# A two-layer attention and FFN kernel on one core: one fixed instruction order replaced by another

## What is computed

```
q, k, v = xs @ Wq, xs @ Wk, xs @ Wv                 # per segment of 128 tokens
sq, sk = elu(q) + 1, elu(k) + 1
att_mem = sq @ mem / (sq @ z)                       # the memory before this segment
mem, z = mem + sk.T @ v, z + sum(sk)                # carried from segment to segment
att = gate * att_mem + (1 - gate) * softmax(q @ k.T / 8) @ v
x = layernorm(x + att @ Wo)
x = layernorm(x + relu(x @ Q(W1).T + b1) @ Q(W2).T + b2)
# Q(W) = clip(round(W / (mean|W| + 1e-5)), -1, 1)
```

## Time and profile before

| | us |
|---|---|
| median of 3 runs | 1915.3 (1911.3 to 1917.6) |
| the profiled execution | 1912.87 |
| its span | 1910.9 |
| PE busy | 1855.7 (97%) |
| DVE busy | 1449.1 (76%) |
| ACT busy | 1006.1 (53%) |
| POOL busy | 794.7 (42%) |

### The profile page before, as it was taken

One profiled execution on the slowest core, in us unless ns is written; L12 is line 12 of the kernel. 1 busy time (PEld: TensorE's weight loads), 2 busy tenths in 40 slices (PEclk: granted clock), 3 DMA queues, 4 the chain that ended last, 5 costly groups with the idle time before them and its releaser, 6 DMA issues.

```text
span 1910.9 us, 44707 instructions
## 1 busy us (share of the span) xinstructions
PE 1855.7 (97%) x16575; PEld 1311.8 (69%) x16575; DVE 1449.1 (76%) x2969; ACT 1006.1 (53%) x2426; POOL 794.7 (42%) x790
## 2 busy tenths in 40 slices
PE   5689999999999999999999999999999999999998
PEld 3566677766777766677766677766677766677765
DVE  7867777777777787777777877777777777777774
ACT  5755555555554555554555554545555645555541
POOL 1813344443344444344444344444345444344443
PEclk9889999999999999999999999999999999999999
DMA  8412333223333233233223333323333322333110
GB/s 270 123 23 46 58 61 66 52 49 59 62 59 65 49 53 61 58 60 65 54 45 64 61 59 64 64 38 60 61 59 63 67 38 59 61 58 62 36 23 23
DMA packets 556422, 117.49 MB, mean 61 GB/s; under 512 B 529824, under 2 KB 533808, under 8 KB 555696
## 3 DMA queue, kind: packets, MB, share of 16 engines
q1 hardware_dynamic: 556208, 114.64, 29.4%
HBM read 50.54 MB, written 16.80 MB: 35 GB/s over the span
## 4 chain that ended last, share of the span: by engine, by line
PE 80%; SPq 7%; DVE 6%; DMA 3%; issue 2%; ACT 1%; POOL 1%; DVEq 0%; POOLq 0%; ACTq 0%
PE bank L431 12%; PE bank L430 12%; PE bank L444 8%; PE bank L445 8%; SPq L1551 7%; PE bank L280 6%; PE bank L282 6%; PE bank L281 6%; PE bank L413 3%; PE bank L411 3%; PE bank L412 3%; PE bank L368 3%; DMA amax_row<-amax_dram 2%; PE bank L294 2%; PE bank L347 2%
## 5 line engine op out<-in xcount | busy, mean ns | idle before, releaser
L430 PE MATMUL bank<-yt,w1t 128*128 128x256 f16 x2048 | 453.9, 273 | 0.0
L431 PE MATMUL bank<-yt,w1t 128*128 128x256 f16 x2048 | 453.9, 273 | 0.0
L1141 ACT ACTIVATE prob<-bank,exp_bias,gscalars 128x128 f32<-128x128 f32 x512 | 227.6, 455 | 356.6 <-DVE exp_bias L723 347.7
L444 PE MATMUL bank<-w2t,arena 128*128 128x512 f16 x1024 | 388.4, 379 | 0.0
L445 PE MATMUL bank<-w2t,arena 128*128 128x512 f16 x1024 | 388.1, 379 | 0.0
L1187 ACT ACTIVATE arena<-bank,b_scaled,wscalars 128x256 f32<-128x256 f32 x512 | 262.9, 569 | 213.4 <-PE bank L431 156.3
L858 DVE CAST arena<-arena 128x512 f16<-128x512 f32 x256 | 154.8, 605 | 89.9 <-ACT arena L1187 89.1
L1317 POOL TENSOR_TENSOR att_mem<-att_mem,gate_in 128x512 f32<-128x512 f32 x60 | 83.1, 1385 | 330.1 <-DVE att_mem L762 318.7
L430 PEld LDWEIGHTS bank<-yt,w1t 128*128 128x128 f16 x2048 | 200.5, 98 | 23.3 <-issue 0.3
L431 PEld LDWEIGHTS bank<-yt,w1t 128*128 128x128 f16 x2048 | 200.3, 98 | 22.7
L1395 POOL TENSOR_TENSOR arena<-arena 128x512 f16<-128x512 f32 x128 | 155.3, 1213 | 87.6 <-DVE arena L858 87.6
(11 more groups left out here) (191 smaller groups left out, 4392.9 us busy)
## 6 DMA issues: line engine op xcount, KB each, us to landing
rows<-in_L_attn_x SPq DMA_DIRECT2D x32, 512.0 KB, 3.6
out_rows<-rows SPq DMA_DIRECT2D x64, 256.0 KB, 2.3
x_blocks<-in_L_attn_x SPq DMA_DIRECT2D x248, 64.0 KB, 2.8
sk<-sk_t SPq DMA_DIRECT2D x480, 32.0 KB, 2.0
att_dot<-att_mem SPq DMA_DIRECT2D x480, 32.0 KB, 2.0
y_blocks<-rows SPq DMA_DIRECT2D x480, 32.0 KB
arena<-in_L_ffn_W SPq DMA_DIRECT2D x6, 1024.0 KB, 5.5
w2t<-in_L_ffn_W SPq DMA_DIRECT2D x2, 1024.0 KB, 13.3
```

The costliest lines, as they stand in the source:

```text
L430: pe.matmul(ps[:, c], w1t[:, k, cols], yt[:, g % 2, :, k], start=k == 0, stop=False)
L431: ins = pe.matmul(ps[:, c], w1t[:, k, cols], yt[:, g % 2, :, KT + k], start=False, stop=k == KT - 1)
L444: pe.matmul(banks[own][:], h_hi[:, f, toks], w2t[:, f, :], start=f == 0, stop=False)
L1141: ins = act.activation(prob[:, t, at], ps[:, c], ACT.Exp, scale=gcol(g, G_EXP), bias=exp_bias[:, t, at:at + 1], accum_out=row_sum[:, t, h: ...
```

## The change

The five engines' loops are written in another order. No instruction is added or removed, with one exception that is no work: DVE's `turn_x` now also waits for the maximum of the same group, which stands ahead of it in the same queue. Line numbers of the changed kernel are one or two off.

The core of the diff, cut to the parts that matter for the steps below:

```diff
+                dve.wait_ge(sem["amax"], g + 1)
                 dve.transpose(x_blocks[:, t], x_blocks[:, t]).then_inc(sem["xturn"], 1)
...
+                if g == 0:
+                    turn_max(1)
+                    spread_max(1)
                 ffn_up(g - 2, 1)
...
+                if g == 1:
                     for n in range(0, 4):
                         turn_w(n)
...
+                read_memory(g, 1)
+                ffn_up(g - 1, 0)
                 attend(g, 1)
-                ffn_up(g - 1, 0)
```

More of the change, by code:

```diff
@@ L548, in _ @@
+                scores(g, 0)
+                project_out(g - 1, 1)
+                ffn_down(g - 2, 0, 0)
                 project_v(g, 0)
-                ffn_down(g - 2, 0, 0)
+                ffn_down(g - 2, 0, 1)
                 project_v(g, 1)
+                scores(g, 1)
+                turn_p(g, 0, 0)
                 if g == 0:
                     turn_bias_max()
-                turn_p(g, 0, 0)
-                ffn_down(g - 2, 0, 1)
+                ffn_down(g - 2, 0, 2)
+                turn_y(g - 1, 0)
@@ L568, in _ @@
+                turn_y(g - 1, 1)
                 turn_p(g, 1, 1)
+                attend(g, 0)
                 ffn_down(g - 2, 1, 2)
[L570 to L573 removed]
                 ffn_down(g - 2, 1, 3)
[L575 to L578 removed]
                 read_memory(g, 1)
[L580 to L585 removed]
+                ffn_up(g - 1, 0)
@@ L1014, in _ @@
                     threshold(1)
-                p_split(g, 0, 0)
-                v_split(g, 1)
-                score_max(g, 1, 0)
-                read_scale(g, 0)
                 score_max(g, 1, 1)
-                residual(g - 2, 0, 1)
                 if g == 0:
@@ L1023, in _ @@
                         compare(n)
+                p_split(g, 0, 0)
+                residual(g - 2, 0, 1)
+                scale_sums(g, 0)
+                read_scale(g, 0)
+                p_split(g, 0, 1)
+                normalise(g - 2, 0, 1)
+                turn_y(g - 1, 0)
+                if (g + 1) % (LIVE * NSEG) < LIVE and LIVE * NSEG <= g + 1 < NG:
+                    reset_memory((g + 1) // (LIVE * NSEG), place(g + 1)[2])
+                yt_lo(g - 1, 0)
+                turn_y(g - 1, 1)
+                p_split(g, 1, 0)
+                yt_lo(g - 1, 1)
+                all_max(g + 1)
+                att_scale(g, 0)
+                x_scale(g + 1, 0)
+                p_split(g, 1, 1)
+                read_scale(g, 1)
+                x_scale(g + 1, 1)
                 invert_sums(g, 1)
-                scale_sums(g, 0)
+                x_scale(g + 1, 2)
+                if g == 0:
+                    scalars(0, 3)
+                x_scale(g + 1, 3)
                 scale_sums(g, 1)
-                turn_y(g - 1, 0)
-                all_max(g + 1)
-                p_split(g, 0, 1)
-                x_scale(g + 1, 0)
+                scalars(g + 1, 0)
+                att_scale(g, 1)
+                scalars(g + 1, 1)
+                h_split(g - 1, 0)
+                xt_lo(g + 1, 0)
+                scalars(g + 1, 2)
                 if g == 0:
@@ L1051, in _ @@
                         compare(n)
-                att_scale(g, 0)
-                read_scale(g, 1)
+                residual(g - 2, 1, 1)
                 if g == 0:
@@ L1227, in _ @@
             for g in range(NG + 2):
+                if g == 1:
+                    for n in range(12, 16):
+                        put_w(n)
                 if g == 0:
-                    w_sum(1, 1)
-                h_relu(g - 2, 4)
+                    gates()
+                h_relu(g - 2, 1)
+                h_relu(g - 2, 2)
+                if g == 0:
+                    w_split("v", 0)
+                if g == 1:
+                    for n in range(16, 20):
+                        put_w(n)
+                if g == 0:
+                    w_split("v", 1)
+                qk_split(g, "k", 0)
+                h_relu(g - 2, 3)
                 if g == 1:
@@ L1276, in _ @@
                         put_w(n)
-                p_split(g, 1, 0)
-                yt_hi(g - 1, 0)
+                xt_hi(g + 1, 1)
                 if g == 0:
@@ L1617, in _ @@
                     load_x(1)
+                move_att(g)
+                if g == 0:
+                    load_ffn_w(2, 2)
                 put_out(g - 2, 1)
```

310 lines of the change are left out of this document (134 added, 176 removed).

## The result

| | before | changed |
|---|---|---|
| median | 1915.3 us (5 runs, 1911.3 to 1917.6) | 1936.1 us (5 runs, 1934.7 to 1936.8) |
| ratio | | 1.0116, 95% interval 1.0099 to 1.0133 |
| profiled execution, its span | 1912.87, 1910.9 | 1936.11, 1934.2 |
| late excess in 28 periods | 9.9 us | 2.7 us |
| undisturbed period | 56.77 us | 57.63 us |

A second comparison of the same two kernels gave 1.0121 (1.0106 to 1.0136): 1936.2 against 1912.5. The forecast of 1907 and its range up to 1917 both missed.

What follows compares the result with a forecast made beforehand. PE, busy for 97% of the span, was taken as the bound, with a 56.77 us floor per group. 1912.9 - 9.5 (late landings) + 3.5 (opening) = 1907 us; range 1901 to 1917.

Steps and rivals of the forecast that it cites:

- (b): Turn of the group: ACT's relu(0), both xt_hi and relu(1) in a row cost PE nothing, with 0.45 us slack.
- (c): Other moved waits (memory add, k and q splits, at_lo, h_rest): 0.9 us or more of slack each, costing nothing.
- The slower rival: At the group's turn a late x_scale delays ACT's relu(1); PE waits 0.6 us in all 30 groups: 1925 us, chance 0.08.
- (a) The landing: DVE reads the returned maximum later, behind p_split(1,0), so late DMA transfers stop delaying groups: gain 9.5 us.
- The 0.4 allowed for leftovers: Part of the 9.9 us late-group excess expected to remain after DVE reads the returned row later: 0.4 us.
- (d) The opening: Before the regular groups: later first k projection and slower turning of FFN weights, costing 3.5 us, bounds -1 and +9.
- the cheap opening: Rival: POOL compares alone in the opening, each falling from 1.97 to 1.57 us; 1901.5 us, chance 0.10.
- (e) The tail: Last two turns, without k, q, v: PE always fed, so no cost, 0 to 1 us.

## Why the prediction was wrong

**The floor of a period: the step that failed.** "Since the change moves instructions and removes none, 56.77 us stays the floor of a group." It rose by 0.87. Two terms were missing.

First, 0.53 us from steps (b) and (c). Step (b), on the turn of the group, prices ACT and PE and has no term for DVE's h_split and `xt_lo` in front of the k projection, 7.0 us into the turn. The second `xt_lo` ended at 7.2 (663.20, with the turn's start at 655.98), and the k projection waited, 0.38 us in every turn. 3.0 of these 7.2 us are the lengthening beside gate_mix and add_bias: h_split took 3.08, 1.11 in the kernel before (+2.0), and the first `xt_lo` 1.75, 0.73 beside a quiet POOL (+1.0). The scaling of the sums ahead of them (L746) is lengthened, too. Step (c) put the slack of the other waits at 0.9 us or more; of these, the q split was planned for 25.0 and the scores for 26.4, and they came at 26.9 and 27.1, with 0.145 us of waiting. No rival held this, although the prediction had the rule in hand and weighed it, for the opening alone and only with its effect on POOL. The slower rival looked at the right place, the turn of the group, and at the wrong engine: PE never waited for a relu.

Second, 0.34 us from PE's own order: one more stretch of half-array matmuls, at 0.25, and transposes directly behind such a stretch, some 0.05 in two places. This was counted at nothing. The 0.25 were moved into the kernel before and measured; the 0.05 are read from rows (four transposes take 0.49 us directly behind the scores, 0.44 elsewhere), and the versions without either come to 56.76 and 56.82 only after a subtraction. The rows of before contain most of it: `scores(g,1)` took 0.68 us up to `read_memory`, `scores(g,0)` 0.78 up to a projection, and `read_memory` 0.99 behind scores and 1.04 behind attend.

**(a) The landing: right.** Forecast -9.5 us; the excess fell from 9.9 to 2.7 (1.9 in its second profile: 1762.05 - 146.34, less 28 x 57.635), and the move alone, put into the kernel before, took 9.1 and 12.4 us off. The 0.4 allowed for leftovers was 2 us too small. One of its readings was off: of the two waits it ascribes to the splits of the probabilities, 3.9 us are booked to them, the 3.6 to no other engine ("issue" in the earlier trace rows).

**(d) The opening: the rows right, the end 1.7 us short.** Forecast and measured: k at 24.7 and 24.52; POOL's last compare at 107.4 and 108.2; the first row maximum of group 1 at 115.8 and 115.77; turn 2 at 135.6 and 137.3. POOL's 16 compares took 1.96 us in the mean, 1.91 before, so the cheap opening did not come. The loss lies behind the row maximum, and what caused it is not shown. Four waits of PE follow there, 1.68, 1.16, 0.73 and 1.09 us, and the granted clock is 0.72 from 130 to 140 us; but the kernel before has 5.7 us of waits in the same stretch and was at the lower clock level for longer, 10.2 us against 6.8:

```profile
104.16 4.08 POOL L1407 TENSOR_SCALAR yt<-arena,wscalars 128x512 f16<-128x512 f32 x2 [1.22 <-PE bank L266]
...
115.77 0.66 DVE L718 TENSOR_REDUCE row_max<-bank 128x4 f32<-128x512 f32 x1
...
130.00:140.00 10.00, 9.94 (x101) 8.83 (x102) 7.70 (x23) 5.78 (x12) 2.92 (x3) 0.72 0.26 45
```

**(e) The tail:** forecast 0 to 1, measured 1.5.

**The sum** with measured terms: 1912.9 - 7.2 + 4.8 + 24.3 + 1.5 = 1936.3, where 1936.1 was measured. Without the missing term it would have been 1912.

## What to carry to other kernels

A reordering does not leave durations alone. Before a new order is priced, write for each DVE instruction of the kinds that were held up here (below) which POOL instruction it will start beside, and give it the rest of that one on top; what is then on the path must be looked at again. And when a change bundles a cure with a new order of everything, try the cure alone: two calls moved on one engine gave the whole 9 to 12 us.

Keep matmuls that use half the array together, and ask of each that is moved forward whose bank it takes.

## What the runs showed of the hardware

- DVE's CAST, TENSOR_TENSOR, SCALAR_TENSOR_TENSOR and TENSOR_SCALAR of 128x512 with all tensors in SBUF, started while POOL was busy, took the rest of POOL's instruction plus their own time, less 0.13 (CAST, L858), 0.14 (TENSOR_TENSOR, L861), 0.18 (SCALAR_TENSOR_TENSOR, L673) or 0.26 us (TENSOR_SCALAR, L840), with hardly any spread. For L858: alone 0.41 us, beside POOL 1.35 in the mean.
- Some DVE instructions with all tensors in SBUF were not lengthened beside POOL: STREAM_TRANSPOSE 0.70 us (L847, L812) and BATCH_NORM_STATS2 0.69 (L831), either way. Nor was one that reads a PSUM bank: 0.68 us either way for L774.
- POOL waits as well: `add_bias` took 1.71 us where it started during DVE's L861, 1.28 in the kernel before.
- Going from full-array matmuls to half-array ones cost 0.09 to 0.10 us, and going back about as much, with no wait in the records.
- A wait of 1.79 us brought PE's granted clock down to 1.2 GHz in 24 of 29 turns and left it alone in 5 (a longer one, 2.13, brought it down as well); waits of 1.10 us did so in 1 of 30. What decides between them was not found.
